# Feed-forward on one Trainium2 core: the third layer's product moved to tokens on the partitions, its scales as a row

## The reference, cut to what matters

```python
def _L0_ffn_ref(x, w1_w, w1_s, w2_w, w2_s, h1_w, h1_s, h2_w, h2_s, w3_w, w3_s):
    def _tlin(x, w, s):
        return jnp.einsum('bsi,oi->bso', x, w) * s
    h = jax.nn.silu(_tlin(x, w1_w, w1_s)) * _tlin(x, w2_w, w2_s)      # 128 -> 512
    h = jax.nn.gelu(_tlin(h, h1_w, h1_s), approximate=False)          # 512 -> 512
    h = jax.nn.gelu(_tlin(h, h2_w, h2_s), approximate=False)          # 512 -> 512
    return _tlin(h, w3_w, w3_s)                                       # 512 -> 128
x = x + _L0_attn_a_ref(_layernorm(x, axis=-1), ...)
x = x + _L0_ffn_ref(_layernorm(x, axis=-1), ...)
x = x + _L0_attn_b_ref(_layernorm(x, axis=-1), ...)
x = x + _L0_ffn_ref(_layernorm(x, axis=-1), ...)
```

## Time and profile before

| | |
|---|---|
| median of 3 runs | 695.62 us (693.09 to 697.49) |
| the profiled execution | 692.88 us, span of the core 691.1 us |
| mean granted clock of TensorE | 0.992 of full speed |
| PE busy | 641.8 us (93%) in 4764 matmuls |
| weight loads | 452.6 us (65%) in 4764 |
| DVE, ACT, POOL busy | 470.6 (68%), 443.6 (64%), 423.5 us (61%) |

### The profile page before, as it was taken

How to read it: one execution, slowest core, us unless ns; L and a number is a source line. 1 busy time by engine, 2 the same in 40 slices (tenths; PEclk the granted TensorE clock), 3 DMA queues, 4 the chain that set the end, 5 groups by cost and what they waited for, 6 DMA issues and landing times.

```text
span 691.1 us, 14147 instructions
## 1 busy us (share of the span) xinstructions
PE 641.8 (93%) x4764; PEld 452.6 (65%) x4764; DVE 470.6 (68%) x925; ACT 443.6 (64%) x781; POOL 423.5 (61%) x456
## 2 busy tenths in 40 slices
PE   3799997999999999998999999998889999999997
PEld 2456665777787786664555555555457777787785
DVE  6477777855677587466888888877577755677511
ACT  3688877665656664555767767766755665656664
POOL 4455455677777766442464564555547876777773
PEclk9999999999999999998999999999999999999999
DMA  6333234000000002631666666662220000000001
GB/s 198 78 85 96 64 76 50 1 1 1 0 0 0 1 1 92 220 118 58 220 192 224 211 220 214 225 223 86 83 94 18 2 15 16 15 15 0 17 16 31
DMA packets 35588, 56.60 MB, mean 82 GB/s; under 512 B 5072, under 2 KB 10192, under 8 KB 35536
## 3 DMA queue, kind: packets, MB, share of 16 engines
q1 hardware_dynamic: 35344, 55.66, 26.4%
q10 hardware_dynamic: 192, 0.26, 0.1%
HBM read 27.08 MB, written 24.38 MB: 74 GB/s over the span
## 4 chain that ended last, share of the span: by engine, by line
PE 64%; ACT 7%; DVE 6%; issue 4%; DMA 3%; POOL 0%; ACTq 0%; SPq 0%; DVEq 0%; POOLq 0%
PE banks L232 61%; ACT b_prob L1570 4%; DVE xn L185 2%; PE banks L1017 1%; PE banks L224 1%; DVE f_gate L1132 1%; DMA b_o_dram<-b_o 1%; DMA f_h_lo<-b_k_dram 1%; DVE f_hidden L1139 1%; ACT f_g_hi L1088 1%; DVE f_h_hi L1136 1%; DMA f_h_hi<-b_negative_max 1%; DMA b_k_dram<-b_k_lo 1%; PE banks L1365 1%; ACT f_tanh L1079 0%
## 5 line engine op out<-in xcount | busy, mean ns | idle before, releaser
L1203 POOL TENSOR_TENSOR f_g_lo<-f_gelu,f_g_hi 128x512 fp32r<-128x512 f32 x127 | 162.8, 1291 | 53.3 <-ACT f_g_hi L1088 52.7
L1087 ACT ACTIVATE f_gelu<-banks,cols 128x512 f32<-128x512 f32 x128 | 88.3, 690 | 127.1 <-PE banks L232 105.1
L1669 DVE TENSOR_REDUCE b_segment_max<-banks 128x6 f32<-128x768 f32 x128 | 120.1, 950 | 28.1 <-PE banks L232 27.6
L1786 POOL TENSOR_SCALAR_AFFINE_SELECT b_prob<-b_prob 128x512 f32<-128x512 f32 x128 | 81.8, 640 | 91.2 <-ACT b_prob L1570 90.5
L232 PE MATMUL banks<-f_g_hi,whi 128*128 128x512 f32 x320 | 130.4, 407 | 2.2 <-POOL f_g_lo L1203 1.7
L232 PE MATMUL banks<-f_g_lo,whi 128*128 128x512 f32 x320 | 126.7, 396 | 0.0
L1570 ACT ACTIVATE b_prob<-banks 128x768 f32<-128x768 f32 x128 | 102.4, 807 | 37.5 <-PE banks L232 37.2
L1196 POOL TENSOR_TENSOR f_h_lo<-f_hidden,f_h_hi 128x512 fp32r<-128x512 f32 x60 | 77.6, 1293 | 58.3 <-DVE f_hidden L1139 50.5
L232 PE MATMUL banks<-f_h_hi,whi 128*128 128x512 f32 x256 | 104.1, 407 | 2.8 <-ACT f_g_hi L1088 2.0
L232 PE MATMUL banks<-f_h_lo,whi 128*128 128x512 f32 x256 | 101.4, 396 | 0.0
L1088 ACT ACTIVATE f_g_hi<-banks,cols 128x512 fp32r<-128x512 f32 x128 | 87.4, 683 | 0.0
(11 more groups left out here) (127 smaller groups left out, 1047.6 us busy)
## 6 DMA issues: line engine op xcount, KB each, us to landing
f_h_hi<-b_q_dram SPq DMA_DIRECT2D x16, 512.0 KB, 4.1
f_h_lo<-b_k_dram SPq DMA_DIRECT2D x16, 512.0 KB, 5.2
b_o_dram<-b_o SPq DMA_DIRECT2D x8, 1024.0 KB, 4.4
b_q_dram<-b_q_hi SPq DMA_DIRECT2D x16, 256.0 KB, 3.2
b_k_dram<-b_k_hi SPq DMA_DIRECT2D x16, 256.0 KB, 2.9
w_stage<-in_wF SPq DMA_DIRECT2D x8, 352.0 KB, 3.4
b_q_dram<-b_q_lo SPq DMA_DIRECT2D x8, 256.0 KB, 3.4
b_k_dram<-b_k_lo SPq DMA_DIRECT2D x8, 256.0 KB, 3.3
```

Of the source, the lines that this page charges most:

```text
L1087: nc.scalar.activation(gf[c % 2][:, :], z_bank[c % 2], ACT.Gelu, scale=scale).then_inc(s_gf, 1)
L1203: nc.gpsimd.tensor_tensor(lo[:, c, :], gf[c % 2][:, :], hi[:, c, :].bitcast(F32), ALU.subtract).then_inc(s_glo[c % 2], 1)
L1669: nc.vector.reduce_max(seg[:, g, s, 2 * p:2 * p + 2, :], first_pass[:, 2 * p:2 * p + 2, 0:3 * P].rearrange("p b (c k) -> p b c k", c=3), A ...
L1786: nc.gpsimd.affine_select(out=pr, in_=pr, compare_op=ALU.is_ge, fill=0.0, base=0, pattern=[[0, 4], [1, P]], channel_multiplier=-1).then_in ...
```

## The change

The third layer's product has its operands exchanged: a tile of 128 tokens of `f_g_hi` or `f_g_lo` is stationary, and 128 columns of `w3` are moving. The result has tokens on the partitions at once. `yT`, `pe_yT` and `act_down` go. The scales stand in `rows` as a row copied to all partitions, and VectorE multiplies `y_bank` by it into a new tile `scaled`, then adds `scaled` to `X`. PE now waits for `s_done` of the block before ahead of each third-layer product, since VectorE reads `y_bank` in its place. One accumulation group covers the whole bank: `start` is set on the first of the 32 products alone, `stop` on the last.

```diff
--- before.py
+++ after.py
@@ -50,11 +50,11 @@
 
 COLS = {}
 for _name, _n in (("s1", KC), ("s2", KC), ("h1s", KC), ("h2s", KC), ("b_content", 1), ("b_spatial", 1), ("b_swapped", 1),
-                  ("bq_b", 1), ("bk_b", 1), ("freq", 1), ("exponent", 1), ("sign", 1), ("factor", 1), ("w3s", 1)):
+                  ("bq_b", 1), ("bk_b", 1), ("freq", 1), ("exponent", 1), ("sign", 1), ("factor", 1)):
     COLS[_name] = (sum(n for _, n in COLS.values()), _n)
 N_COLS = sum(n for _, n in COLS.values())
 
-ROWS = ("bv", "bo", "bv_b", "bo_b")
+ROWS = ("bv", "bo", "bv_b", "bo_b", "w3s")
 
 
 class Block:
@@ -934,7 +934,7 @@
             hhi, hlo = h_split
             g1hi, g1lo = g1_split[F]
             g2hi, g2lo = g2_split
-            th, uu, hf, gf, yT, sc = (ffn[k] for k in ("th", "u", "hf", "gf", "yT", "sc"))
+            th, uu, hf, gf, scaled, sc = (ffn[k] for k in ("th", "u", "hf", "gf", "scaled", "sc"))
             GATES_BEHIND = ((0,), (1,), (), (2, 3))
             t_bank = banks[0]
             a_bank, b_bank = [banks[1], banks[3]], [banks[2], banks[4]]
@@ -954,7 +954,6 @@
             s_glo = [sem(f"{F}_gelu_lo{i}") for i in range(2)]
             s_y = sem(f"{F}_projected")
             s_ys = sem(f"{F}_scaled")
-            s_yt = sem(f"{F}_scaled_transposed")
             s_done = sem(f"{F}_x_updated")
 
 
@@ -1003,19 +1002,18 @@
                         beside(c)
 
             def pe_down(pe, b, parts):
+
                 t = b.t
+                wait(pe, s_done, t)
                 for kc in range(KC):
                     pe.wait_ge(s_glo[kc % 2], 4 * t + 2 + kc // 2 + 1)
-                    for n, (i, j) in enumerate(parts):
-                        last = mm(y_bank, ffn["w3"][i][:, kc, :], (g2hi, g2lo)[j][:, kc, :],
-                                  start=kc == 0 and n == 0, stop=kc == KC - 1 and n == len(parts) - 1)
+                    for s in range(TILES):
+                        at = slice(s * P, (s + 1) * P)
+                        for n, (i, j) in enumerate(parts):
+                            last = mm(y_bank[:, at], (g2hi, g2lo)[j][:, kc, at], ffn["w3"][i][:, kc, :],
+                                      start=kc == 0 and s == 0 and n == 0,
+                                      stop=kc == KC - 1 and s == TILES - 1 and n == len(parts) - 1)
                 last.then_inc(s_y, 1)
-
-            def pe_yT(pe, b):
-                pe.wait_ge(s_ys, b.t + 1)
-                for s in range(TILES):
-                    last = nc.tensor.transpose(y_bank[:, s * P:(s + 1) * P], yT[:, s * P:(s + 1) * P], ident[:, :])
-                last.then_inc(s_yt, 1)
 
             def pe_T(pe, n, bank=t_bank):
                 norm.pe(pe, n, bank)
@@ -1035,8 +1033,6 @@
                             nxt["pe_front"](pe, b, "first", c)
 
                     def beside_second(c):
-                        if before and c == 0:
-                            pe_yT(pe, b.after(-1))
                         if two and c == 2:
                             pe_T(pe, n2)
                         if is_block(b, 0):
@@ -1046,8 +1042,6 @@
 
                     pe_hidden(pe, b, False, parts, beside_first)
                     if before:
-                        if not one:
-                            pe.wait_ge(s_done, b.t - 1)
                         pe_down(pe, b.after(-1), parts)
                     pe_hidden(pe, b, True, parts, beside_second)
 
@@ -1058,10 +1052,7 @@
             def pe_tail(pe, parts, at):
 
                 if at == 0:
-                    pe.wait_ge(s_done, LAST)
                     pe_down(pe, LAST_BLOCK, parts)
-                else:
-                    pe_yT(pe, LAST_BLOCK)
 
 
             def act_xhi(act, n, bank=t_bank):
@@ -1096,8 +1087,6 @@
                         act_tanh(act, n1, c)
                     if nxt:
                         nxt["act_front"](act, b, "first", c)
-                if before:
-                    act_down(act, b.after(-1))
                 for c in range(KC):
                     act_gelu(act, b, True, c)
                     if two and c == 2:
@@ -1105,11 +1094,6 @@
                     if nxt:
                         nxt["act_front"](act, b, "second", c)
 
-            def act_down(act, b):
-                act.wait_ge(s_y, b.t + 1)
-                wait(act, s_yt, b.t)
-                nc.scalar.activation(yT[:, :], y_bank[:, :], ACT.Copy, scale=col("w3s")).then_inc(s_ys, 1)
-
             def act_program(act):
                 nc.scalar.preload_act_table(ACT.Gelu)
                 act_body(act, FIRST_BLOCK, False, True, True)
@@ -1117,7 +1101,7 @@
                 act_body(act, LAST_BLOCK, True, False, False)
 
             def act_tail(act):
-                act_down(act, LAST_BLOCK)
+                pass
 
 
             def dve_xlo(dve, n, bank=t_bank):
@@ -1146,8 +1130,10 @@
                                         ALU.subtract).then_inc(s_hlo[c % 2], 1)
 
             def dve_down(dve, b):
-                dve.wait_ge(s_yt, b.t + 1)
-                nc.vector.tensor_tensor(xblk(b.t), tiles_of(y_bank), xblk(b.t), ALU.add).then_inc(s_done, 1)
+                dve.wait_ge(s_y, b.t + 1)
+                nc.vector.tensor_tensor(scaled[:, :, :], tiles_of(y_bank), row4("w3s"), ALU.mult).then_inc(s_ys, 1)
+                dve.wait_ge(s_ys, b.t + 1)
+                nc.vector.tensor_tensor(xblk(b.t), scaled[:, :, :], xblk(b.t), ALU.add).then_inc(s_done, 1)
 
             def dve_body(dve, b, before, one, two):
                 prev, nxt = link["prev"], link["next"]
@@ -1951,7 +1937,7 @@
         attention_first = attention_a(links[0])
         scope.pop().close()
         g2_split = [sb(f"f_g2_{part}", [P, KC, TOK], F32R) for part in ("hi", "lo")]
-        ffn["yT"] = sb("f_yT", [P, TOK])
+        ffn["scaled"] = sb("f_scaled", [P, TILES, E])
         ffn_first = feed_forward("f1", links[1])
         attention_second = attention_b(links[2])
         ffn_second = feed_forward("f2", links[3])
@@ -2062,9 +2048,9 @@
         qkv_b[0][:, None], qkv_b[1][:, None], np.broadcast_to(A("nrope_freq"), (P, 1)),
         (-(feature % quarter) / quarter).astype(f)[:, None],
         (np.where(feature < quarter, -1, 1) * factor).astype(f)[:, None],
-        factor[:, None], Fn("w3_s")[:, None]], 1)
+        factor[:, None]], 1)
     io["rows"] = np.broadcast_to(
-        np.concatenate([A("bv"), A("bo"), qkv_b[2], Bn("out_b")])[None, :], (P, len(ROWS) * E))
+        np.concatenate([A("bv"), A("bo"), qkv_b[2], Bn("out_b"), Fn("w3_s")])[None, :], (P, len(ROWS) * E))
     return {k: np.ascontiguousarray(v) for k, v in io.items()}
 
 
```

## The result

| | before | after |
|---|---|---|
| median of four runs each, us | 694.50 (693.09 to 697.49) | 708.58 (706.89 to 712.42) |
| profiled execution, its span, us | 692.88, 691.1 | 712.42, 710.7 |

The ratio is 1.022 (95%: 1.019 to 1.026), so the change costs some 14 to 15 us. The execution in the profile was the longest of its four, and the one of before was shorter than any of its four, so the spans differ by 19.6: the profile shows where the time lies, the runs how much it is.

A forecast was written before the change was run, and what follows sets the result against it. The prediction took TensorE's instruction count times pace to bound the feed-forward blocks. Its terms, 16.4 + 0.3 + 1.6 + 0.1 = +18.4 us, put on the median 695.62, gave 714.0 us, with a range of 707 to 723.

The forecast's parts named there:

- The pair: Third-layer product: each weight load plus 128-column product takes 0.112 us, load exposed; 32 take 3.58 us a block.
- The rival of hidden loads: Third-layer product: loads run ahead under the stream, 0.059 us each, 688.2 us in all; chance 0.04.
- the one in between near 0.08: Third-layer product: load and product together near 0.08 us, about 700 us in all; chance 0.04.
- The 81 ns of the Trainium skill: Third-layer product: documented 81 ns per load and 128-column product, giving +0.27 us a block and about 699.5 us.
- The block: Thirteen feed-forward bodies on TensorE's chain: +1.26 us each (1.10 to 1.78), +16.4 us together.
- Nobody is waited for: Feed-forward layers before the change: time is PE's instruction count times pace, 21.7 us a block, 0.237 per 512-column product.
- Body 6: Sixth body of f1: PE's 1.44 us stall before `b_k_lo` shortens, so +0.3 us, or +1.3 if the add runs long.
- The start of the second attention: Going into that attention: PE's wait for the scaled result vanishes, its wait for `xn` grows; +1.6 us.
- The tail: Kernel's end: later products, then multiply and add replacing scaling, transposes and add; -0.1 to +0.2 us, 0.1 taken.
- The add that reads SBUF alone: VectorE's add behind the down product: 0.7 to 1.7 us a block, covered by VectorE's idle time.
- rival 4: VectorE falls behind: the SBUF add is long everywhere and its cover gone, 14 us more, 728 us; chance 0.04.
- Rival 3: PE's clock falls in each of 14 third-layer stretches, about +3.3 us each, 46 us, 760 us; chance 0.04.

The follow-up runs named there:

- experiment 2: Changed kernel with 16 loads a block, each followed by 256 columns of `w3`, high parts alone; 693.38 us, 0.999 of the kernel before.
- experiment 5: Changed kernel with the third layer's operands alone in bf16, still 32 pairs a block; 691.85 us, 0.998 of the kernel before.
- experiment 8: Kernel before with only VectorE's order changed, last gate ahead of the four `xn` steps; 688.57 us, 0.992 of the kernel before.
- experiment 1: Changed kernel with the low part of the activations left out of the third layer, 16 pairs instead of 32; 693.08 us, 0.999 of the kernel before.
- experiments 4: Changed kernel with one unread activation of 0.69 us a block put back on ScalarE; 709.94 us, 1.022 of the kernel before.
- experiment 9: Changed kernel with only VectorE's order changed, last gate ahead of the four `xn` steps; 709.26 us, 1.022 of the kernel before.
- experiment 10: Changed kernel with half of the pairs, and VectorE adding `y_bank` to `X` in one step without scales; 686.31 us, 0.989 of the kernel before.

## Why the prediction was right, point by point

**The pair: right.** Predicted 0.112 us, measured 0.1116, so 32 pairs cost 3.57 where 3.58 stood. The reason given, a weight load of 128 columns that 128 moving columns can't hide, is shown: doubling the columns adds 0.008 us (experiment 2), and shortening the load halves the pair (experiment 5). The rival of hidden loads, and the one in between near 0.08, are out. The rival that VectorE's two steps or the new wait for `s_done` cost the time is out too: with them in place and half the pairs gone, the block fell to 22.13. The 81 ns of the Trainium skill (page "TensorE: Matmul & The Clock Gate", section "Back-to-back issue gap"), which the prediction weighed, isn't what this kernel has in either type: fp32r pairs run at 112 ns, bf16 at 55 to 56.

**The block: mis-sized, 1.07 us in eight blocks and not 1.26.** The step that failed is the sentence "Nobody is waited for". TensorE's own sum of before is 88 products at 0.234, 20.6, and 0.87 of transposes: 21.48 (experiment 8 runs at just that). The block took 21.67, so 0.19 of it was a wait, and the change first had to fill that. It stands in the trace of before, in the timeline of all engines, which the prediction doesn't use:

```profile
226.13 1.29 POOL L1196 TENSOR_TENSOR f_h_lo<-f_hidden,f_h_hi 128x512 fp32r<-128x512 f32 x1 [2.52 <-DVE f_hidden L1139]
...
227.38 2.54 POOL L1203 TENSOR_TENSOR f_g_lo<-f_gelu,f_g_hi 128x512 fp32r<-128x512 f32 x2
...
228.75 0.69 ACT L1087 ACTIVATE f_gelu<-banks,cols 128x512 f32<-128x512 f32 x1 [1.43 <-POOL f_g_lo L1203]
...
230.07 0.19 PEld L232 LDWEIGHTS banks<-f_h_hi,whi 128*128 128x128 f32 x1 [0.32 <-ACT f_g_hi L1088]
```

Even the earlier trace rows alone gave it away. Its 16 products in 3.74 are 0.234 each, its 72 in 17.09 are 0.237; I put both down as one pace, 0.237. The difference, 72 x 0.0036 = 0.26 us, is no pace but a wait. The views show none, since a product's record is 0.40 long where starts are 0.234 apart: the end of one record covers the start of the next, and TensorE reads as 100% busy through a gap of 0.1 us.

The five other bodies had no such wait to fill. Ahead of body 1 of each layer the gap of 1.33 us stands in both kernels (142.14 to 143.47 before, 142.95 to 144.29 after); in body 7 of f1 and in bodies 6 and 7 of f2 VectorE makes no `xn` steps. There the change cost 1.2 to 1.3, the predicted 1.26. Thirteen bodies are 14.7 us, where the prediction had 16.4.

After, the two chains stand the other way: TensorE's own sum is 22.73 and the second chain is near the 22.13 that it has in experiment 1. That the change is longer by TensorE's work alone is what experiments 4 and 9 confirm.

**Body 6: right in its mechanism.** The stall was to fall from 1.44 us to under 0.6; it fell to 0.26. From the start of the down product to the end of the stall it is 6.26 us (271.50 to 277.76), where before had 6.18 (265.22 to 271.40): +0.1, where +0.3 was predicted. The prediction counted back to 265.8 for that start, by pace; the 16 products from there held a wait. Ahead of the down product the block is 0.14 shorter, the second chain's wait once more, so the stretch from transposes to transposes (249.35 to 276.15) comes to -0.1.

**The start of the second attention: the wait turned, as predicted, 0.4 us smaller.** The wait for the scaled result went, and the one for `xn` rose from 1.53 to 2.37 us. The 3 us came, but not in one piece: TensorE waits 0.66 for ScalarE's `b_prob` (until 321.00), does score products that had stood behind the scaled result, and then waits the 2.37. From the start of the down product to the transposes of `xn` it is 8.7 us (315.43 to 324.15) instead of 7.5 before, +1.2 for a predicted +1.6. Of the 0.4 between them, about 0.15 is VectorE's tail, as its timeline shows, and most of the rest the way from `xn` to TensorE, 1.57 us (322.58 to 324.15) for a predicted 1.7:

```profile
320.38 0.96 DVE L1655 TENSOR_REDUCE b_segment_max<-banks 128x6 f32<-128x768 f32 x1 [2.19 <-PE banks L232]
321.26 0.68 DVE L1134 TENSOR_TENSOR f_scaled<-banks,rows 128x512 f32<-128x512 f32 x1
321.97 0.69 DVE L1136 TENSOR_TENSOR X<-f_scaled,X 128x512 f32<-128x512 f32 x1
322.58 1.43 DVE L185 TENSOR_SCALAR xn<-X,mv,rstd 128x128 f32<-128x128 f32 x4
```

The starts run closer than the durations add up: from the reduction's start to `xn` it is 322.58 - 320.38 = 2.20 where 2.35 stood.

**The tail: right.** Its sum was -0.1 to +0.2. From the start of the down product to the end of the add it takes 5.13 us (702.47 to 707.60), where before took 5.2 (683.01 to 688.22):

```profile
706.19 0.69 DVE L1134 TENSOR_TENSOR f_scaled<-banks,rows 128x512 f32<-128x512 f32 x1 [1.46 <-PE banks L232]
706.91 0.69 DVE L1136 TENSOR_TENSOR X<-f_scaled,X 128x512 f32<-128x512 f32 x1
```

**VectorE: within its bounds.** The add that reads SBUF alone was given 0.7 to 1.7 us. Its group after (min, median, max in ns):

```profile
L1136 DVE TENSOR_TENSOR X<-f_scaled,X x16: 691/1229/1359, 162.6 to 706.9; 128x512 f32 x8, 128x512 f32<-128x512 f32 x8
```

In the change it is covered, as rival 4 needed it not to be. In experiment 1, where TensorE has less to do, it is worth 0.46 us a block through GpSimd (experiment 10). The cover is thin, and the prediction named only VectorE's queue as what stood behind it.

**The sum.** 14.7 - 0.1 + 1.2 - 0.1 = 15.7 us, beside 14.1 between the medians and 15.3 by the ratio (13.0 to 17.8). The forecast of 714.0 is 5.4 too high: 1.7 of the blocks, 0.4 at the attention, 0.4 at body 6, 0.2 of the tail, and 1.1 because before's median was 694.50 with the fourth run and not 695.62; 1.6 is left, which four runs don't tell from nothing. The 708.58 lies 1.6 above the low end of the stated range, and under the 711.3 that the prediction gave as the forecast's own low end. What kept it inside are the 2 to 3 us that were added for the spread of the runs and the clock, so that part is luck. The pace of the pair is not.

**What stays open.** The spans of the profiles differ by 3.9 us more than this sum: 1.7 in the stretch where the clock drops at 507 (3.4 us at half the clock with TensorE busy throughout would cost about that), 1.1 in the second attention, 0.8 ahead of f1's first body, 0.2 behind the last add. Among after's four runs the span follows the mean clock, from 710.7 at 0.989 to 705.2 at 0.994, so at least a part comes and goes from run to run. No experiment was aimed at why the clock fell there. Rival 3, a drop in every block, is out, since the clock stands at 1.00 in both long windows. In the profile of experiment 9 one drop does begin inside a third-layer product, the one at the attention's start (at 317.0). TensorE had waited 0.73 us, until 314.53, and no run says whether the product had a part in it.

## What to carry to other kernels

Exchanging the operands of a product to save a transpose keeps the columns but multiplies the loads, so price the pair and not the columns: here a 128-column pair in fp32r costs 0.112 us against 0.059 for its share of a long product, and the exchange loses, while in bf16 it costs 0.055 and wins, once no other chain holds the block. A chain of waits that stays on one engine isn't proof that it is never late: divide its pieces by their counts, and where two pieces of the same instruction have two paces, the slower one holds a wait. And before taking work from the engine that looks bound, take it away in an experiment with nothing else changed: 0.44 us gone here from a steady block without effect showed a second chain, and in such a block the order of two steps on VectorE, one number in the code, was worth more (0.19). Count the odd bodies as well: where the wait isn't there to fill, the price is another.

## What the runs showed of the hardware that was not expected

**VectorE and GpSimd make each other wait when both have their operands in SBUF.** In experiment 1, timelines of the two engines:

```profile
208.16 1.24 DVE L1134 TENSOR_TENSOR X<-f_scaled,X 128x512 f32 x1 [0.16 <-DVE f_scaled L1132]
```

```profile
207.54 1.30 POOL L1180 TENSOR_TENSOR f_h_lo<-f_hidden,f_h_hi 128x512 fp32r<-128x512 f32 x1 [2.53 <-DVE f_hidden L1121]
208.80 2.97 POOL L1187 TENSOR_TENSOR f_g_lo<-f_gelu,f_g_hi 128x512 fp32r<-128x512 f32 x2
```

The add takes 1.24 us instead of the 0.69 that it takes at the kernel's end, with GpSimd idle. It ends at 209.40, so a run of 0.69 would have begun at 208.71, close to where GpSimd's first step ends (its record ends at 208.84). GpSimd's next step in turn takes 1.76 us instead of 1.29, from 208.80 to 210.56, which is what it would be if it could begin only near 209.3, about when the add ends. So the times fit one engine standing until the other's instruction is over, at a cost of about half a microsecond to each. The Trainium skill, page "SBUF — State Buffer", section "SBUF: two separate sides", states this: a VectorE operation with two SBUF inputs and a GpSimd operation that reads SBUF contend for a port pair that one of them holds for its whole instruction. The trace agrees, and experiment 10 agrees from the other side: with VectorE's operand in PSUM the same GpSimd step takes 1.30.

**The load's price depends on the type.** Where loads follow one another, 128 columns of fp32r occupy the path for 0.11 us, and of bf16 for 0.056 at most. The Trainium skill, page "TensorE: Matmul & The Clock Gate", section "Weight-path perf modes", has weight loads about twice as fast for types other than fp32 when there are 128 of them; the trace agrees, with fp32r on the side of fp32.

**The load's price depends on the clock too.** In experiment 9's profile the granted clock falls to 0.50 at 317.0, inside the 32 pairs of the attention's start:

```profile
316.84 0.28 PE L232 MATMUL banks<-whi,f_g_hi 128*128 128x128 f32 x1
...
318.17 0.41 PE L232 MATMUL banks<-whi,f_g_lo 128*128 128x128 f32 x1
318.38 0.41 PE L232 MATMUL banks<-whi,f_g_hi 128*128 128x128 f32 x1
```

Behind the fall the pairs start 0.213 apart (317.32 to 320.30) instead of 0.1116. So a pair that waits for its load costs nearly twice as much at half the clock.
